# Attention: the weight transposes of two steps issued together, eight in a row, ahead of the score and value products of both steps

## What is computed

```python
q = (x @ wq).reshape(B, L, 16, 128);  k, v: 4 heads, from x (L = 256) and from the context (T = 4096)
q, k = rope(rms_norm(q)), ...                       # k_full, v_full: 4352 keys
scores = jnp.einsum('blhd,bmhd->bhlm', q, k_full) * scale + mask
probs = jax.nn.softmax(scores, axis=-1)
out = jnp.einsum('bhlm,bmhd->blhd', probs, v_full)
return out.reshape(B, L, 16 * 128) @ wo
```

## Time and profile before

| | |
|---|---|
| median of the executions | 1056.17 us |
| the profiled execution | 1059.17 us |
| its span (first to last instruction) | 1057.1 us |
| mean granted TensorE clock | 0.995 of full speed |
| TensorE (PE) busy | 1039.6 us |
| VectorE (DVE) busy | 777.4 us |
| ScalarE (ACT) busy | 601.4 us |
| the 272 steps on TensorE | from 258.7 to 740.7 us |

### The profile page before, as it was taken

How to read it: one execution, slowest core, us unless ns; L and a number is a source line. 1 busy time by engine, 2 the same in 40 slices (tenths; PEclk the granted TensorE clock), 3 DMA queues, 4 the chain that set the end, 5 groups by cost and what they waited for, 6 DMA issues and landing times.

```text
span 1057.1 us, 15522 instructions
## 1 busy us (share of the span) xinstructions
PE 1039.6 (98%) x5773; PEld 888.1 (84%) x5773; DVE 777.4 (74%) x1659; ACT 601.4 (57%) x1089; POOL 190.0 (18%) x208
## 2 busy tenths in 40 slices
PE   7999999999999999999999999999999999999998
PEld 5888888887888888888888888888776788888887
DVE  5856777649777877777877777787567778777775
ACT  4444343334765566666556666659356466666664
POOL 4644434320000000000000000003132012222221
PEclk9999999999999999999999999999999899999999
DMA  6758676498004130043100440004450285555550
GB/s 233 244 190 289 213 240 193 134 318 289 12 1 163 59 119 1 2 169 105 65 1 8 163 159 17 1 1 181 175 214 1 90 338 181 185 195 188 186 173 21
DMA packets 64156, 145.76 MB, mean 138 GB/s; under 512 B 3889, under 2 KB 42705, under 8 KB 62673
## 3 DMA queue, kind: packets, MB, share of 16 engines
q1 hardware_dynamic: 64080, 144.77, 39.5%
HBM read 108.55 MB, written 36.21 MB: 137 GB/s over the span
## 4 chain that ended last, share of the span: by engine, by line
PE 93%; DVE 4%; ACT 1%; issue 1%; DMA 0%; POOL 0%; DVEq 0%; ACTq 0%
PE bank L546 18%; PE bank L483 16%; PE bank L589 12%; PE bank L566 11%; PE bank L464 10%; PE bank L837 9%; PE bank L591 6%; PE bank L839 4%; PE bank L646 2%; PE bank L493 1%; DVE conv_acc L1115 1%; PE bank L659 1%; PE bank L776 1%; PE bank L727 1%; DVE e_hl L1226 0%
## 5 line engine op out<-in xcount | busy, mean ns | idle before, releaser
L1044 DVE TENSOR_TENSOR pT<-bank,pT 128x512 fp32r<-128x512 f32 x272 | 184.6, 688 | 103.4 <-ACT pT L1453 101.4
L1453 ACT CAST pT<-bank 128x512 fp32r<-128x512 f32 x272 | 156.0, 593 | 142.8 <-PE bank L566 139.6
L589 PE MATMUL bank<-pT,vN 128*128 128x512 f32 (+1 forms) x544 | 225.7, 422 | 0.0
L546 PE MATMUL bank<-kT,qT_hi 128*128 128x512 f32 (+2 forms) x576 | 215.4, 393 | 2.1 <-DVE scores L988 2.1
L988 DVE TENSOR_SCALAR_CACHE_REDUCE scores<-bank 128x512 f32<-128x512 f32 x256 | 173.0, 685 | 2.0 <-PE bank L546 0.2
L566 PE MATMUL bank<-ident,scores 128*128 128x128 f32 x1072 | 161.3, 272 | 0.4 <-DVE pT L1044 0.3
L1424 ACT ACTIVATE scores<-scores,neg_max 128x1024 f32<-128x1024 f32 (+2 forms) x128 | 154.0, 1203 | 6.3 <-DVE neg_max L1000 6.3
L591 PE MATMUL bank<-pT,vN 128*128 128x256 f32 (+1 forms) x544 | 152.5, 280 | 0.0
L483 PE MATMUL bank<-w_ctx_hi,ctx_hl 128*128 128x512 f32 x512 | 145.5, 396 | 6.6 <-ACT ctx_hl L1333 6.6
L837 PE MATMUL bank<-fT_parts,e_hl 128*128 128x512 f32 x400 | 144.6, 398 | 0.1
L566 PEld LDWEIGHTS bank<-ident,scores 128*128 128x128 f32 x1072 | 127.2, 140 | 12.1 <-DVE pT L1044 1.2
(11 more groups left out here) (223 smaller groups left out, 1561.9 us busy)
## 6 DMA issues: line engine op xcount, KB each, us to landing
e_raw<-in_experts SPq DMA_DIRECT2D x51, 768.0 KB, 4.4
k_spill<-k_stage SPq DMA_DIRECT2D x16, 1024.0 KB, 4.5
v_spill<-v_stage SPq DMA_DIRECT2D x16, 1024.0 KB, 8.3
vN<-v_spill SPq DMA_DIRECT2D x16, 1024.0 KB, 5.2
kT<-k_spill SPq DMA_DIRECT2D x15, 1024.0 KB, 5.3
ctx_raw<-in_ctx SPq DMA_DIRECT2D x15, 512.0 KB, 4.1
w_raw<-in_w_qkv SPq DMA_DIRECT2D x6, 1024.0 KB, 5.0
wo_sb<-in_wo SPq DMA_DIRECT2D x4, 1024.0 KB, 9.3
```

What stands on the lines that cost most here:

```text
L546: done = e.matmul(bank[b][:, 0:n], qT[a][:, h, qt * P:(qt + 1) * P], kT[:, w, lo:lo + n], start=m == 0, stop=m == 2)
L589: e.matmul(halves[:, :, q0:L], vN[:, 0, kt, :], ring[:, :, i * L + q0:(i + 1) * L], start=kt == 0, stop=False)
L1044: e.tensor_tensor(ring[:, 1, :], bank[tb][:, :], ring[:, 0, :], ALU.subtract).then_inc(p_lo, 1)
L1453: e.copy(ring[:, 0, :], bank[tb][:, :]).then_inc(p_hi, 1)
```

## The change

The loop over the steps goes by pairs, n0 and n0 + 1 with n0 even. Both steps' transposes are issued first, then the products of n0, then those of n0 + 1. Nothing else is changed; the semaphores that each instruction waits for are the same, and no engine but TensorE has another order.

```diff
-            for h in range(NH):
-                for kk in range(NPAIR):
-                    turn_weights(h, kk)
-                    n = h * NPAIR + kk
+            for n0 in range(0, NH * NPAIR, 2):
+
+                for n in (n0, n0 + 1):
+                    turn_weights(*divmod(n, NPAIR))
+                for n in (n0, n0 + 1):
+                    h, kk = divmod(n, NPAIR)
                     in_turns(plan.in_step[h, kk], weigh(n - LAG) if n >= LAG else None)
                     if kk == SPREAD_AT:
                         spread_sums(h)
```

## The result

The changed kernel takes 1059.44 us in the median (ten runs, 1058.77 to 1060.57), the kernel before beside it 1056.76 us (ten runs, 1055.53 to 1058.68). The ratio is 1.0020, with a 95% interval of 1.0012 to 1.0029: slower by 2.1 us, 1.3 to 3.1. The forecast was 2.9. The two medians are 2.7 us apart, which lies within that interval.

A forecast was written before the change was run, and what follows sets the result against it. TensorE, busy 98% of the span, was taken as the bound. No saving from joined runs plus early waits of 1.5, 0.70 and 0.70 us gave + 2.9 us, from 1056.17 to 1059.1 us; range 1055.0 to 1062.0 us.

The forecast's parts named there:

- the 0.2% that the prediction asks for: Whole kernel: smallest difference told from no change, 2.1 us; under 1054.1 us is faster, over 1058.3 us slower.
- Step 1: TensorE's transposes: 0.11 us each in runs of any length, no fixed price per run, so joining runs saves 0.
- its bound of 0.02 us: Fixed part of a transpose run: at most 0.02 us to either side, 2.7 us either way over 136 pairs.
- Step 2: ScalarE's casts and VectorE's low parts come at nearly today's times; the even step's products start 0.44 us later.
- Step 3: Odd step's transposes ask for the low part of n0 − 2 earlier; it is late at three kinds of place.
- End of even heads: Heads 2 to 14, step 0 of the next head: TensorE waits, 0.21 us each, 7 × 0.21 = 1.5 us.
- Head 0: End of head 0: four products of step 16 no longer fill the wait for step 14's low part, + 0.70 us.
- Head 15: Step 6 of head 15: products of step 5 now stand behind the wait for step 3's low part, + 0.70 us.
- The fixed price of a run: Rival, at each of 136 pairs: a saved price of 0.09 us per run, giving 1046.9 us; chance 0.10.
- More waits than seen: Rival: later evictions and casts add 0.2 us in two places of 14 heads, 5.6 us, 1064.7 us; chance 0.12.
- the covers of 0.36 and 0.4 us: Time left before TensorE would wait: 0.36 us for low parts at odd heads' step 6, about 0.4 for evictions.
- The clock: Rival: longer transpose runs drop TensorE to half speed in steps without scores, 67 us, 1126 us; chance 0.03.

The follow-up runs named there:

- all pairs but nine: The change, with steps kept apart at step 16 of even heads and steps 5 and 6 of head 15: ratio 0.9989, stage 481.51 us.
- the nine alone: The kernel before, with steps joined only at step 16 of even heads and step 5 of head 15: ratio 1.0030, stage 484.97 us.
- both moves on ScalarE: The change with one exponential per head moved behind step 14's cast: 1.0001; separately, with head 14's output cast moved behind step 3 of head 15: 1.0014.
- the runs cut up: The kernel before, each step's four transposes split two and two (ratio 1.0001) or each put ahead of its own value product (1.0157).
- one by one: The kernel before, each step's four transposes each put ahead of a value product of its own: ratio 1.0157, stage 499.53 us.
- the control with the exponential moved: The kernel before, with one exponential per head moved from behind step 13's cast to behind step 14's: ratio 0.9995, stage 482.07 us.

## Why the prediction was right

**Direction and size.** Forecast + 2.9 us, measured + 2.0 in the stage and + 2.1 (1.3 to 3.1) by the ratio of the times. In the stage it is the early waits, + 3.04, less what joined pairs save, 1.05. Whether the whole is slower by more than the 0.2% that the prediction asks for, the runs don't settle: the ratio lies on that bound, though well clear of no change. That the median of 1059.44 us is so near the forecast 1059.1 is luck: the sum was 0.9 us too large, and the kernel before took 0.6 us more beside the changed one (1056.76) than in the three executions that the forecast started from (1056.17).

**Step 1, no saving per run.** Held within its bound of 0.02 us, for eight in a row too, but the saving is not nothing: about 0.008 us for each joined run (1.05 us over 136 pairs, and again 0.95 in the kernel with all pairs but nine). It is the term that made the sum 0.9 too large: 3.04 of waits less 1.05. I took it as 0, which starts given to 0.01 us could not tell from 0.008. And it is an average, not an even price: by the spacing of starts, steps 2 and 3 together are 0.04 us shorter than before in heads 4, 8 and 12, and 0.01 longer in heads 2, 6 and 10.

**Step 2, deliveries unchanged.** Held: VectorE's low part of step 14 in head 8 begins 272.76 us behind step 0 of head 0 in the changed kernel and 271.90 before, 0.86 later, just as TensorE itself was behind there by then (0.85).

**Step 3, the wait that moves ahead.** Held in all three kinds of place, and is shown as the cause by the nine alone and by both moves on ScalarE. End of even heads: forecast 0.21 us, measured 0.22. Head 0: 0.70 forecast, 0.75 measured. Head 15: 0.70 and 0.75. In the last two the four products of a step, 0.70, no longer fill a wait that was there before.

**A slip in the reading.** The window of the earlier trace rows at full clock holds eight steps without scores, not nine; nothing in the sum hangs on it.

**The rivals.** The fixed price of a run is refuted by the runs cut up. More waits than seen: none in the changed kernel; the covers of 0.36 and 0.4 us held. Their mechanism is real, as the evictions with one by one and the uncovered step 8 show. The clock stayed at 1.00 from 300 to 700 us, with up to eight transposes in a row and the same share of them as before. The Trainium skill (TensorE: Matmul & The Clock Gate, "Part 4: PE-mode transpose") says that transposes don't count as busy for the clock gate as products do; in this mix no fall followed, and a longer stretch of transposes alone was not tried.

## What to carry to other kernels

Where an engine has no idle time, moving its instructions has no gap to fill. It can make them a little cheaper side by side (here 1.05 us over 136 pairs), and it asks for others' results at other times (here 3.04 us of waits); with the early waits taken away, the pairs won. So list each wait in the moved group, with when it is asked now, when it will be, and when the result is there; a place that already waits today is the dearest, since the work moved behind the wait no longer fills it. A long first product behind a group is no proof of a price per group: compare groups of different length by the spacing of starts.

## What I had not expected of the hardware

- Joining two runs of transposes saves about 0.008 us on average, while cutting one up costs 0.002. Both are small against 0.11 for a transpose, but they are not the same number, and no run here says why. It stays open.
- Executions of one kernel differ by more than this change is worth. In thirteen of the kernel before, taken beside the runs cut up, the spans were 1054.2 to 1055.1 us where the mean granted clock was 1.000, and 1056.3 to 1058.0 where it was 0.995. In the two profiles compared above, the lower clock was a stretch of 20 us far behind the stage in question (0.83 against 1.00 from 830 to 850 us). A stage at full clock repeats far better: the control with the exponential moved kept its 0.28 us ahead of the kernel before, to 0.01 us, from step 1 of head 1 to step 5 of head 15.
